# Layer 1's constants and halves prepared inside layer 0, and the last batch's normalisers fetched by two queues

## The chip, the cores and the metric

The kernel runs on one NeuronCore of one Trainium2 chip. The metric is the device time of one execution in microseconds, taken as the median over runs.

## What is computed

Two transformer layers are applied to x of shape (4, 1024, 128), in float32. The reference, cut to what matters:

```python
xn = layernorm(x)
x = x + L0_attn(xn) + L0_ffn(xn)   # 16 heads of 8, one shared key/value; SwitchHead: 8 heads, 8 experts, top 2
xn = layernorm(x)
x = x + L1_attn(xn) + L1_ffn(xn)   # FAVOR+ linear attention; 8 experts, top 2, plus a shared expert
return x
```

In layer 0's attention each head's output is softmax(q k) v, so each head's sum over keys has to be divided by its own denominator before the output projection with Wo. Layer 1's attention needs q, k and v as products of xn with Wq, Wk and Wv, and its experts need to know which tokens chose which expert.

## The kernel before

All 32 tiles of 128 tokens stay in SBUF as `x`, and `xnT` holds the normalised tokens transposed. A product that needs more precision than one float32r pass is made in three (`matmul3`, lines 91 to 98): both operands are split into an upper half (`upper`, a rounded copy) and a lower half (`lower`, what the rounding left, line 86).

**Layer 0** (`layer0`) runs 32 steps, 8 per batch, in one software-pipelined loop whose order is written out by hand for each engine; step i works on one SwitchHead head and two attention heads of batch i // 8. Around that loop each engine has the work of a batch's boundary (`batch_work`). The sums of the attention heads, undivided, go out to DRAM (`store_sums`, on ScalarE's queue), and with them a ninth row, the denominators. When a batch is through:

- `load_dens` (L685, SyncE's queue) fetches the denominators into `dens`, and `invert_dens` (L1369, VectorE) inverts them.
- `load_o` stores the inverses to DRAM (L692), fetches the sums into `o_in` (L699, 16 DMAs) and then the inverses, each repeated over 8 partitions, into `rden_in` (L705, 16 DMAs), all on SyncE's queue. Each of these 32 DMAs brings 32 KB in rows of 256 bytes.
- `divide_o` (L775, GpSimd, two halves) multiplies them into `oT`, `project_out` (L421, TensorE) applies Wo, `add_attn` (L1377, VectorE) adds to `x`, `token_moments` (L1384) takes the statistics, `normalise_out` (L1291), `turn_xo` (L386), `keep_xoT` (L977) and the routing (L431, L1403, `choose_experts`, `mix`) follow.

For batches 0 to 2 this lies beside the steps of the next batch. For batch 3 nothing is left beside it: after the loop every engine has a short tail written out by hand. VectorE's tail is the routing of batch 2 first, and then `invert_dens(B - 1)` and the rest. The halves `xs` of a batch's tokens are made by `upper_x` (ScalarE, L963) and `lower_x` (GpSimd, L86) one batch ahead, for layer 0 only.

**Layer 1** (`main1`) is a second block, entered by all engines together behind a barrier. SyncE issues the loads of 15 constants and weights there (L1717); TensorE, ScalarE and VectorE wait for all 15 (`loaded`). Then VectorE makes the upper halves of the weights (L82, `wh` and `w1`), GpSimd the lower halves (L86), ScalarE and GpSimd the halves `xh` of three batches of tokens (L2303, and L86 with 12 pieces). TensorE's first product is `project_in(0, 0)`, behind `w_split` and `x_split`. In slot 1 of batch 0 it counts the tokens of each expert (`count_places`, L1962 and L1963), and VectorE's `rank_tokens` (L2086 to L2111) gives each token its place; TensorE's next ring buffer waits for that (`ranked`), and so does GpSimd, which sends the rows out (`send_rows`, L2459).

## Time and profile before

| what | us |
|---|---|
| median of 3 runs | 3246.56 |
| lowest and highest of them | 3239.7, 3247.78 |
| the profiled execution's own time | 3217.92 |
| its span | 3216.1 |
| layer 0 ends, layer 1 starts (first DMA of layer 1) | 2643.34 |

The span is the time from the first to the last instruction of the profiled execution; 1.82 us of its own time lie around it. That execution was 28.6 us faster than the median of the runs shown, so differences are worked out within it. The profile's page gives the busy time of each engine over the whole span; the stretch around 2600 to 2680 us is read from the timeline, in order of time, and from windows, which give the same sums for a stretch.

### The profile page before, as it was taken

How to read it: one execution, taken by the hardware profiler on the slowest of the kernel's cores; microseconds unless marked ns; L12 is line 12 of the kernel's file. 1: busy time of each engine (PE TensorE's matmuls, PEld its weight loads, DVE VectorE, ACT ScalarE, POOL GpSimd, SP SyncE). 2: the span in 40 equal slices, each digit the busy share in tenths (PEclk: the TensorE clock that was granted, in tenths of full speed). 3: DMA queues.
4: the chain of work that ended last, by engine and by line, in shares of the span. 5: the costliest groups of instructions: out<-in, count | busy, mean ns of one | idle time of the engine just before them, and what ended most of it. 6: DMA issues, size and time to landing. Idle time of an engine off the chain costs nothing. (4 is left out here: it accounts for less than half of the span.)

```text
span 3216.1 us, 51790 instructions
## 1 busy us (share of the span) xinstructions
PE 3007.4 (94%) x17486; PEld 2085.3 (65%) x17486; DVE 2392.0 (74%) x4547; ACT 1617.6 (50%) x3269; POOL 1840.3 (57%) x2283
## 2 busy tenths in 40 slices
PE   4999999999999999999999999999999937898997
PEld 2666666666666666666666666666666625566674
DVE  7888888888888888888888888888878534144343
ACT  1555555555555555555555555555555612344534
POOL 2556666666666666666666666666666426334330
PEclk7999999999999999999999999999999968899999
DMA  5000000101100011001000110010000021123222
GB/s 165 20 22 22 21 22 22 39 23 34 37 22 23 22 31 31 22 22 35 28 22 22 31 31 25 20 44 25 22 22 21 2 49 58 59 85 105 86 76 84
DMA packets 139561, 124.62 MB, mean 39 GB/s; under 512 B 28122, under 2 KB 121828, under 8 KB 139204
## 3 DMA queue, kind: packets, MB, share of 16 engines
q1 hardware_dynamic: 126836, 88.78, 10.0%
q0 software_dynamic: 10160, 30.17, 3.0%
q10 hardware_dynamic: 2304, 2.36, 0.4%
q8 instruction: 143, 2.34, 0.3%
q14 instruction: 118, 0.97, 0.1%
HBM read 97.48 MB, written 29.30 MB: 39 GB/s over the span
## 5 line engine op out<-in xcount | busy, mean ns | idle before, releaser
L1172 DVE TENSOR_REDUCE m_peaks<-m_ring 128x1 f32<-128x512 f32 x1024 | 640.9, 680 | 116.2 <-PE m_ring L270 110.0
L926 ACT ACTIVATE m_expA<-m_ring 128x512 f32<-128x512 f32 x1024 | 538.6, 602 | 370.9 <-PE m_sums L358 179.5
L817 POOL TENSOR_TENSOR m_vprod<-m_vprod 128x512 f32<-128x512 f32 x256 | 354.9, 1386 | 510.7 <-DVE m_vprod L1185 509.3
L826 POOL TENSOR_TENSOR m_oprod<-m_oprod 128x512 f32<-128x512 f32 x256 | 328.1, 1282 | 282.3 <-DVE m_oprod L1252 282.2
L897 ACT ACTIVATE m_prob<-m_ring,m_negs 128x512 f32<-128x512 f32 x512 | 347.0, 684 | 241.6 <-DVE m_negs L1219 241.4
L321 PE MATMUL m_ring<-m_probT,m_vs 128*128 128x256 f32 x2048 | 467.4, 381 | 0.0
L321 PEld LDWEIGHTS m_ring<-m_probT,m_vs 128*128 128x128 f32 x2048 | 384.5, 190 | 79.5 <-issue 27.2
L1213 DVE TENSOR_REDUCE m_negs<-m_ring 128x1 f32<-128x512 f32 x512 | 340.3, 685 | 93.6 <-PE m_ring L98 93.1
L1252 DVE TENSOR_TENSOR m_oprod<-m_ring,m_go 128x512 f32<-128x512 f32 x512 | 341.3, 685 | 57.6 <-PE m_ring L98 53.7
L1185 DVE TENSOR_TENSOR m_vprod<-m_ring,m_gate 128x512 f32<-128x512 f32 x512 | 336.5, 683 | 46.0 <-POOL m_vs L819 23.9
L907 ACT ACTIVATE m_probT<-m_ring 128x512 f32<-128x512 f32 x512 | 285.0, 598 | 58.0 <-PE m_ring L309 54.3
L309 PEld LDWEIGHTS m_ring<-k_ident,m_prob 128*128 128x128 f32 x2048 | 235.3, 141 | 82.8 <-ACT m_prob L897 31.4
L309 PE MATMUL m_ring<-k_ident,m_prob 128*128 128x128 f32 x2048 | 283.8, 276 | 4.7 <-ACT m_prob L897 3.8
L358 PE MATMUL m_sums<-m_expA,m_v 128*32 128x512 f32 x2048 | 273.2, 605 | 2.0 <-ACT m_expA L926 2.0
L270 PE MATMUL m_ring<-m_ks,m_qs 32*128 32x512 f32 x1024 | 211.8, 491 | 30.8 <-DVE m_qs L1164 28.2
L96 PE MATMUL m_ring<-m_wvs,m_xs 128*128 128x512 f32 x512 | 230.5, 450 | 4.1 <-POOL m_wvs L86 2.8
L96 PE MATMUL m_ring<-m_xs,m_yT 128*128 128x512 f32 x512 | 227.9, 445 | 3.3 <-ACT m_prob L897 0.9
L96 PE MATMUL m_ring<-m_wos,m_ctxT 128*128 128x512 f32 x512 | 224.8, 439 | 5.6 <-ACT m_expA L926 2.0
L343 PE MATMUL m_ring<-m_qs,m_ks 32*128 32x512 f32 x1024 | 205.2, 483 | 11.7 <-DVE m_vprod L1185 8.0
L917 ACT ACTIVATE m_ctxT<-m_ring 128x256 fp32r<-128x256 f32 x128 | 49.1, 384 | 314.6 <-PE m_ring L321 314.6
L98 PE MATMUL m_ring<-m_wvs,m_xs 128*128 128x512 f32 x512 | 203.9, 398 | 0.0
L97 PE MATMUL m_ring<-m_wvs,m_xs 128*128 128x512 f32 x512 | 203.5, 397 | 0.0
(293 smaller groups left out, 5646.9 us busy)
## 6 DMA issues: line engine op xcount, KB each, us to landing
m_wraw<-in_v_w SPq DMA_DIRECT2D x32, 512.0 KB, 4.1
m_qf<-q_dram SPq DMA_DIRECT2D x128, 128.0 KB, 2.7
m_wraw<-in_o_w SPq DMA_DIRECT2D x32, 512.0 KB, 4.2
q_dram<-m_kf SPq DMA_DIRECT2D x24, 256.0 KB, 3.0
listed<-in_pad SPq DMA_DIRECT2D x6, 897.0 KB, 11.8
m_xg<-listed SPq DMA_DIRECT2D x39, 138.0 KB, 2.2
m_rows<-answers SPq DMA_DIRECT2D x8, 512.0 KB, 4.2
sums_dram<-m_sumsT ACTq DMA_DIRECT2D x128, 18.0 KB
```

The source lines that it names most:

```text
L96: pe.matmul(out, wh, xh, start=True, stop=False)
L309: last = pe.transpose(ps[:, c * P:(c + 1) * P], prob[t % 2][:, (4 * h + c) * P:(4 * h + c + 1) * P], ident[:, :])
L321: last = pe.matmul(ps[:, 0:2 * P], vs[n % 2][:, k, :], probT[g % 2][:, k, :], start=(k == 0), stop=(k == TPB - 1))
L817: vchain(pool.tensor_tensor(vprod[:, 0:512], vprod[:, 0:512], vprod[:, 512:1024], ALU.add))
L826: ochain(pool.tensor_tensor(op[:, 0:512], op[:, 0:512], op[:, 512:1024], ALU.add))
L897: act.activation(prob[t % 2][:, c * 512:(c + 1) * 512], ring.home["scores", n, t, c][:, :], ACT.Exp, bias=neg[t % 2], accum_out=den[n % 2] ...
L907: act.activation(probT[g % 2][:, 4 * h:4 * h + 4, (t % 2) * P:(t % 2 + 1) * P], ring.home["probT", n, t, h][:, :].rearrange("p (c q) -> p ...
L926: act.activation(expA[hh][:, c * 512:(c + 1) * 512], ring.home["scT", n, k, hh, c][:, :], ACT.Exp)\
L1172: v.tensor_reduce(peaks[:, t, hh, c:c + 1], ring.home["peaks", n, t, hh, c][:, :], AX.X, ALU.max)\
L1185: v.tensor_tensor(vprod[:, c * 512:(c + 1) * 512].rearrange("p (e d) -> p e d", e=4), ring.home["values", n, t, c][:, :].rearrange("p (e d ...
L1213: v.tensor_reduce(half_neg[:, t % 2, c:c + 1], ring.home["scores", n, t, c][:, :], AX.X, ALU.max, negate=True)\
L1252: v.tensor_tensor(oprod[t % 2][:, c * 512:(c + 1) * 512].rearrange("p (e d) -> p e d", e=4), ring.home["outputs", n, t, c][:, :].rearrange ...
```

## The change

What is done in layer 1 before its first product moves into layer 0. The 15 constants are loaded by SyncE in step 29 (`load_layer1`), into `spare`, a tile that held the normalised tokens `xn` and the gates' scratch before. Their halves are made by VectorE alone in layer 0's tail (`split_layer1`), into `wvs`, which layer 0 no longer needs then. `upper_x` and `lower_x` run once more in layer 0, for batch 0's tokens of layer 1, in steps 28 and 29; those of batches 1 and 2 are made in layer 1, between ScalarE's `keep_kT` and `keep_qT` and behind GpSimd's `square_k`. TensorE, ScalarE and GpSimd start layer 1 without a wait for loads.

For the last batch the inversion comes first in VectorE's tail, the sums are fetched by SyncE without a wait for it, the store of the inverses and half of their loads go to ScalarE's queue, the division is shared by GpSimd and VectorE, and the statistics of a half are taken as soon as that half is added.

```diff
+def layer1_consts(spare):
+
+    at, out = 0, {}
+    for name, rows, shape in (("wraw", P, (3, D)), ("woT", P, (D,)), ("bqk", P, (2,)), ("bv", P, (D,)), ("proj", P, (256,)),
+                              ("pick", P, (256,)), ("half", P, (P,)), ("vmask", P, (2, 32)), ("w2", P, (HT, D)),
+                              ("b1", P, (HT,)), ("b2", EM + 2, (D,)), ("ws1", P, (HID,)), ("rank", P, (P + 17 + NG + NT,))):
+        n = math.prod(shape)
+        view = spare[0:rows, at:at + n]
+        out[name] = view.rearrange("p (a b) -> p a b", a=shape[0]) if len(shape) == 2 else view
+        at += n
+    return out
...
-        st, xn, kf = norm_memory(m), m.sbuf("xn", [P, TPB, D]), m.sbuf("kf", [P, 512])
+        st, xn, kf = norm_memory(m), spare[:, 0:T].rearrange("p (t d) -> p t d", t=TPB), m.sbuf("kf", [P, 512])
         tiny = m.sbuf("tiny", [P, 1])
-        g_v, g_one, g_c, g_other = (m.sbuf(f"g_{n}", [P, 64, ES]) for n in ("v", "one", "c", "other"))
+        g_v, g_one, g_c, g_other = (spare[:, k * 512:(k + 1) * 512].rearrange("p (g e) -> p g e", e=ES) for k in range(2, 6))
...
+        def load_rden(eng, b, parts):
+
+            eng.wait_ge(rden_stored, 16 * (b + 1))
+            rden_of = rden_dram[b % 2].rearrange("(h c) (g u) -> c g h u", c=2, g=HD)
+            for c in parts:
+                for g in range(HD):
+                    rows = slice(64 * c + HD * g, 64 * c + HD * (g + 1))
+                    eng.dma_start(rden_in[rows, :, :], rden_of[c, g, :, :].partition_broadcast(HD)).then_inc(o_loaded, 16)
...
                 def load_o(b):
                     if b not in batches:
                         return
-                    sp.wait_ge(dens_inverted, b + 1)
-                    sp.dma_start(rden_dram[b % 2].rearrange("g (s r) -> g s r", s=4), dens[:, :]).then_inc(rden_stored, 16)
                     if b:
                         sp.wait_ge(o_divided, 2 * b)
                     sums_of = sums_dram[b % 2].rearrange("h (i c) k (g u) -> c g k (h i) u", i=2, g=HD)
...
                         for g in range(HD):
                             rows = slice(64 * c + HD * g, 64 * c + HD * (g + 1))
                             sp.dma_start(o_in[rows, :, :], sums_of[c, g, 0:HD, :, :]).then_inc(o_loaded, 16)
-                    sp.wait_ge(rden_stored, 16 * (b + 1))
-                    rden_of = rden_dram[b % 2].rearrange("(h c) (g u) -> c g h u", c=2, g=HD)
-                    for c in range(2):
-                        for g in range(HD):
-                            rows = slice(64 * c + HD * g, 64 * c + HD * (g + 1))
-                            sp.dma_start(rden_in[rows, :, :], rden_of[c, g, :, :].partition_broadcast(HD)).then_inc(o_loaded, 16)
+                    if b < B - 1:
+                        sp.wait_ge(dens_inverted, b + 1)
+                        sp.dma_start(rden_dram[b % 2].rearrange("g (s r) -> g s r", s=4), dens[:, :]).then_inc(rden_stored, 16)
+                    load_rden(sp, b, range(2) if b < B - 1 else (0,))
...
+                def load_layer1():
+                    sp.wait_ge(xn_turned, 2 * B)
+                    sp.wait_ge(gates_ready, 2 * B)
+                    for dst, src in (
+                        (w["wraw"][:, 0, :], a["wkT"]), (w["wraw"][:, 1, :], a["wqT"]), (w["wraw"][:, 2, :], a["wvT"]),
+                        (w["woT"], a["woT"]), (w["bqk"], a["bqk"]), (w["bv"], a["bv1"].partition_broadcast(P)),
+                        (w["proj"], a["proj"]), (w["half"], a["half"]), (w["pick"], a["pick"]), (w["vmask"], a["vmask"]),
+                        (w["b2"], a["b2"]), (w["ws1"], a["ws1"]), (w["w2"], a["ws2"]), (w["b1"], a["bs1"]), (w["rank"], a["rank"]),
+                    ):
+                        sp.dma_start(dst, src).then_inc(layer1_loaded, 16)
...
+                    if i == N0 - 3:
+                        load_layer1()
...
                 def lower_x(b):
-                    if b not in batches:
+                    if not 0 <= b <= B:
                         return
                     pool.wait_ge(x_upper, b + 1)
-                    lower(pool, xs[b % 2][:, 1, :], xnT[:, b * T:(b + 1) * T], xs[b % 2][:, 0, :]).then_inc(x_ready, 1)
+                    at = b % B * T
+                    lower(pool, xs[b % 2][:, 1, :], xnT[:, at:at + T], xs[b % 2][:, 0, :]).then_inc(x_ready, 1)
...
                 divide_o(B - 1, 0)
-                divide_o(B - 1, 1)
...
                 def upper_x(b):
-                    if b not in batches:
-                        return
-                    act.wait_ge(xnT_made, 2 * (b + 1))
+
+                    if not 0 <= b <= B:
+                        return
+                    if b < B:
+                        act.wait_ge(xnT_made, 2 * (b + 1))
+                    else:
+                        act.wait_ge(xoT_made, 2)
                     if b >= 2:
                         act.wait_ge(scores_made, 2 * TPB * HS * (b - 1))
-                    act.activation(xs[b % 2][:, 0, :].bitcast(F32R), xnT[:, b * T:(b + 1) * T], ACT.Copy).then_inc(x_upper, 1)
+                    at = b % B * T
+                    act.activation(xs[b % 2][:, 0, :].bitcast(F32R), xnT[:, at:at + T], ACT.Copy).then_inc(x_upper, 1)
...
+                act.wait_ge(dens_inverted, B)
+                act.dma_start(rden_dram[(B - 1) % 2].rearrange("g (s r) -> g s r", s=4), dens[:, :]).then_inc(rden_stored, 16)
+                load_rden(act, B - 1, (1,))
                 routing_exps(B - 2)
                 roots(5 + B - 1, slice(NT - TPB, NT))
...
+                def split_layer1():
+
+                    v.wait_ge(layer1_loaded, 16 * n_layer1)
+                    v.wait_ge(values_made, 16 * N0)
+                    halves = Chain(v, halves_step)
+                    upper(v, w["wh"][:, 0, :, :], w["wraw"])
+                    halves(upper(v, w["w1"][:, 0, :], w["ws1"]))
+                    lower(v, w["wh"][:, 1, :, :], w["wraw"], w["wh"][:, 0, :, :])
+                    lower(v, w["w1"][:, 1, :], w["ws1"], w["w1"][:, 0, :])
+                    v.tensor_scalar(w["bqk"], w["bqk"], DN, None, ALU.mult)
+
+                def divide_last():
+
+                    v.wait_ge(o_loaded, 512 * B)
+                    v.wait_ge(out_made, 2 * (B - 1))
+                    v.wait_ge(xo_turned, 2 * (B - 1))
+                    v.wait_ge(xo_stored, 16 * FILLS + 16 * (B - 1))
+                    heads = slice(8, 16)
+                    v.tensor_tensor(oT[:, :].rearrange("p (u h) -> p h u", h=H0)[:, heads, :], o_in[:, heads, :],
+                                    rden_in[:, heads, :], ALU.mult).then_inc(o_divided, 1)
...
-                    v.wait_ge(attn_added, 2 * (b + 1))
+                    v.wait_ge(attn_added, 2 * b + 1 + pair // 2)
...
+                invert_dens(B - 1)
                 keep_routing(B - 2)
                 choose_experts(B - 2)
                 mix(B - 2)
-                invert_dens(B - 1)
-                add_attn(B - 1, 0)
-                add_attn(B - 1, 1)
-                for pair in range(4):
-                    token_moments(B - 1, pair)
+                split_layer1()
+                divide_last()
+                for q in range(2):
+                    add_attn(B - 1, q)
+                    token_moments(B - 1, 2 * q)
+                    token_moments(B - 1, 2 * q + 1)
...
-        xh = [m.sbuf(f"xh{k}", [D, 2, T]) for k in range(3)]
+        xh = [*xs, m.sbuf("xh2", [D, 2, T])]
...
-                pe.wait_ge(loaded, 16 * n_loads)
-                pe.wait_ge(consts_ready, 2)
...
                 def project_in(b, side, out_sem, kept_sem):
-                    if side == 0:
-                        pe.wait_ge(x_split, b + 1)
-                    if b == 0 and side == 0:
-                        pe.wait_ge(w_split, 1)
+                    if b and side == 0:
+                        pe.wait_ge(x_split, b)
...
-                    v.memset(cum[k][:, 0:4], 0.0)
-                v.wait_ge(loaded, 16 * n_loads)
-                upper(v, wh[:, 0, :, :], wraw[:, :, :]).then_inc(consts_ready, 1)
-                v.tensor_scalar(bqk[:, :], bqk[:, :], DN, None, ALU.mult).then_inc(consts_ready, 1)
-                upper(v, w1[:, 0, :], ws1[:, :]).then_inc(consts_ready, 1)
+                    last = v.memset(cum[k][:, 0:4], 0.0)
+                last.then_inc(consts_ready, 1)
...
-                for b in range(B - 1):
-                    upper_x(b)
                 for b in range(B):
                     for u in range(SLOTS):
                         if u == 0:
                             keep_kT(b)
                         if u == 1:
                             keep_qT(b)
+                        if b == 0 and u < 2:
+                            upper_x(u + 1)
...
-                pool.wait_ge(consts_ready, 1)
-                lower(pool, wh[:, 1, :, :], wraw[:, :, :], wh[:, 0, :, :]).then_inc(w_split, 1)
-                pool.wait_ge(consts_ready, 3)
-                lower(pool, w1[:, 1, :], ws1[:, :], w1[:, 0, :]).then_inc(w_split, 1)
...
+                            if b == 0:
+                                lower_x(1)
+                                lower_x(2)
```

**Where the instructions stand.** Line numbers are those of the kernel they belong to. SyncE's queue at layer 0's end before (m_ names are layer 0's tiles; "waits" are semaphores, m0_ those of layer 0):

```order
L685 DMA m_dens<-sums_dram 128x1x128 [waits m0_rden_stored,m0_sums_stored]
L692 DMA rden_dram<-m_dens 128x128 [waits m0_dens_inverted]
L699 DMA m_o_in<-sums_dram 8x16x64 [waits m0_o_divided]
L699 DMA m_o_in<-sums_dram 8x16x64 x15
L705 DMA m_rden_in<-rden_dram 8x16x64 [waits m0_rden_stored]
L705 DMA m_rden_in<-rden_dram 8x16x64 x15
L711 DMA xn_dram<-m_oT 128x1024 [waits m0_xo_ready]
```

and ScalarE's queue at the same place now:

```order
L976 DMA sums_dram<-m_sumsT 9x512 [waits m0_sums_kept]
L1014 ACTIVATE k_xnT<-m_ring 128x512 [waits m0_x_ready,m0_xo_turned] x2
L1185 DMA rden_dram<-m_dens 128x128 [waits m0_dens_inverted]
L264 DMA m_rden_in<-rden_dram 8x16x64 [waits m0_rden_stored]
L264 DMA m_rden_in<-rden_dram 8x16x64 x7
L1057 ACTIVATE m_lg<-m_lg 128x64 [waits m0_lg_ready]
L981 ACT_TABLE_LOAD
L981 ACTIVATE m_rstd<-m_va 128x8 [waits m0_var_ready]
```

The store of the inverses and 8 of the 16 loads of `m_rden_in` left SyncE's queue for ScalarE's, where they stand ahead of batch 2's routing exponential.

VectorE's tail before:

```order
L1411 TENSOR_TENSOR m_t_sel<-m_t_sel,m_t_q 128x64 [waits m0_mix_step]
L1412 TENSOR_TENSOR m_lg<-m_lg,m_t_first 128x64 [waits m0_mix_step]
L1418 TENSOR_TENSOR m_lg<-m_lg,m_t_sel 128x64 [waits m0_lg_exps]
L1419 TENSOR_REDUCE m_t_m<-m_lg 128x8 [waits m0_mix_step]
L1420 RECIPROCAL m_t_m<-m_t_m 128x8 [waits m0_mix_step]
L1421 TENSOR_TENSOR k_combine<-m_lg,m_t_m 128x8x8 [waits m0_mix_step]
L1369 RECIPROCAL m_dens<-m_dens 128x128 [waits m0_dens_loaded]
L1377 TENSOR_TENSOR k_x<-k_x,m_ring 128x512 [waits m0_x_added,m0_out_made] x2
L1384 BN_STATS m_bn<-k_x 128x6 [waits m0_attn_added]
L1384 BN_STATS m_bn<-k_x 128x6
```

and now (k_spare holds the constants, k_wvs the halves):

```order
L1481 RECIPROCAL m_t_m<-m_t_m 128x8 [waits m0_mix_step]
L1482 TENSOR_TENSOR k_combine<-m_lg,m_t_m 128x8x8 [waits m0_mix_step]
L83 CAST k_wvs<-k_spare 128x384 [waits m0_values_made,m0_layer1_loaded]
L83 CAST k_wvs<-k_spare 128x512
L87 TENSOR_TENSOR k_wvs<-k_spare,k_wvs 128x384 [waits m0_halves_step]
L87 TENSOR_TENSOR k_wvs<-k_spare,k_wvs 128x512
L1420 TENSOR_SCALAR k_spare<-k_spare 128x2
L1429 TENSOR_TENSOR m_oT<-m_o_in,m_rden_in 128x8x64 [waits m0_xo_turned,m0_xo_stored,m0_out_made,m0_o_loaded]
L1438 TENSOR_TENSOR k_x<-k_x,m_ring 128x512 [waits m0_x_added,m0_out_made]
L1445 BN_STATS m_bn<-k_x 128x6 [waits m0_attn_added]
```

The reciprocal has gone from behind the routing to ahead of it (it stands 14 instructions before the first row shown), five instructions on the weights and one half of the division came in, and the statistics follow each addition.

ScalarE at the start of layer 1 before:

```order
L2291 UNCONDITIONAL_BRANCH [waits barrier_Pool_Activation_PE_DVE_SP_release]
L2303 ACTIVATE m_xh<-k_xnT 128x1024 [waits m1_consts_ready,m1_loaded]
L2303 ACTIVATE m_xh<-k_xnT 128x1024 x2
L2311 ACTIVATE m_kT<-m_ring,m_bqk 128x1024 [waits m1_kT_made]
L2319 ACTIVATE m_qT<-m_ring,m_bqk 128x1024 [waits m1_qT_made]
L2362 ACT_TABLE_LOAD
```

and now:

```order
L2332 UNCONDITIONAL_BRANCH [waits barrier_Pool_Activation_PE_DVE_SP_release]
L2347 ACTIVATE m_kT<-m_ring,k_spare 128x1024 [waits m1_kT_made]
L2339 ACTIVATE k_xs<-k_xnT 128x1024
L2355 ACTIVATE m_qT<-m_ring,k_spare 128x1024 [waits m1_qT_made]
L2339 ACTIVATE m_xh<-k_xnT 128x1024
L2400 ACT_TABLE_LOAD
```

The copies of the tokens' halves no longer stand ahead of `m_kT`; two of them stand behind `m_kT` and `m_qT`, and no wait for loads is left.

## Rows read from the trace of the kernel before

**Rows 1.** The page of the profile, part 1: busy us, share of the span, instructions.

```profile
PE 3007.4 (94%) x17486; PEld 2085.3 (65%) x17486; DVE 2392.0 (74%) x4547; ACT 1617.6 (50%) x3269; POOL 1840.3 (57%) x2283
```

**Rows 2.** Timeline, end of layer 0: start us, us, engine line op out<-in xcount [idle before].

```profile
2592.84 0.56 SPq L685 DMA_DIRECT2D m_dens<-sums_dram  x1
...
2596.22 0.23 DVE L1403 TENSOR_TENSOR m_lg<-m_ring,m_gb 128x64 f32<-128x64 f32 x1 [2.02 <-PE m_ring L431]
...
2600.38 0.26 ACT L1020 ACTIVATE m_lg<-m_lg 128x64 f32<-128x64 f32 x1 [6.24 <-DVE m_lg L1412]
...
2601.57 0.94 DVE L1369 RECIPROCAL m_dens<-m_dens 128x128 f32<-128x128 f32 x1
...
2602.93 5.84 SPq L699 DMA_DIRECT2D m_o_in<-sums_dram  x16
...
2608.82 5.93 SPq L705 DMA_DIRECT2D m_rden_in<-rden_dram  x16
...
2619.38 2.52 POOL L775 TENSOR_TENSOR m_oT<-m_o_in,m_rden_in 128x512 f32<-128x512 f32 x2 [21.18 <-DMA m_rden_in<-rden_dram]
...
2621.95 3.78 PE L421 MATMUL m_ring<-m_wo,m_oT 128*128 128x128 f32 x16 [25.77 <-POOL m_oT L775]
```

**Rows 3.** DMA issues of 2585:2660: xcount, KB each, median us to landing.

```profile
m_dens<-sums_dram SPq DMA_DIRECT2D x1, 64.0 KB, 2.3
...
rden_dram<-m_dens SPq DMA_DIRECT2D x1, 64.0 KB, 1.6
```

**Rows 4.** DMA issues of 2089:2106 (same transfer, batch 2).

```profile
rden_dram<-m_dens SPq DMA_DIRECT2D x1, 64.0 KB, 4.3
```

**Rows 5.** Windows: us, busy (x instructions) of each engine, PEclk, DMA share, GB/s.

```profile
2093.00:2095.00 2.00, 2.00 (x14) 0.98 (x14) 2.00 (x4) 0.88 (x2) 0.00 (x0) 1.00 0.67 117
...
2614.00:2616.00 2.00, 0.00 (x0) 0.00 (x0) 0.00 (x0) 0.00 (x0) 0.00 (x0) 0.50 0.72 71
...
2700.00:2750.00 50.00, 44.93 (x447) 32.94 (x448) 12.24 (x18) 23.05 (x27) 34.06 (x35) 1.00 0.19 60
```

**Rows 6.** Timeline, VectorE after the last output projection.

```profile
2625.77 0.69 DVE L1377 TENSOR_TENSOR k_x<-k_x,m_ring 128x512 f32<-128x512 f32 x1 [1.02 <-PE m_ring L421]
...
2626.49 2.05 DVE L1384 BATCH_NORM_STATS2 m_bn<-k_x 128x6 f32<-128x128 f32 x8
```

**Rows 7.** Timeline, the start of layer 1.

```profile
2643.34 0.36 SPq L1717 DMA_DIRECT2D m_wraw<-in_wkT  x1
...
2653.13 0.36 DVE L82 CAST m_wh<-m_wraw 128x384 fp32r<-128x384 f32 x1 [7.92 <-DMA m_rank<-in_rank]
...
2656.12 8.63 POOL L86 TENSOR_TENSOR m_xh<-k_xnT,m_xh 128x256 fp32r<-128x256 f32 x12
...
2659.50 0.77 PE L96 MATMUL m_ring<-m_xh,m_wh 128*128 128x512 f32 x1 [21.35 <-POOL m_xh L86]
```

**Rows 8.** Timeline, layer 1's ranking of tokens and what runs beside it.

```profile
2656.48 0.83 DVE L2078 TENSOR_TENSOR m_qpT<-m_qpT 128x256 f32<-128x256 f32 x1
...
2670.12 1.11 ACT L2319 ACTIVATE m_qT<-m_ring,m_bqk 128x1024 f32<-128x1024 f32 x1 [6.56 <-PE m_ring L98]
...
2671.54 0.42 DVE L2086 COPY m_qpT<-m_ring 128x256 f32<-128x256 f32 x1 [2.11 <-PE m_ring L1963]
...
2671.99 2.26 DVE L2089 TENSOR_TENSOR m_qpT<-m_qpT 128x256 f32<-128x256 f32 x5
...
2680.57 0.24 DVE L2111 TENSOR_SCALAR m_weight_rows<-m_owner,m_rank 128x39 uint32<-128x39 f32 x1
```

**Rows 9.** Timeline, GpSimd and SyncE in layer 0.

```profile
1856.92 2.36 POOL L86 TENSOR_TENSOR m_xs<-k_xnT,m_xs 128x1024 fp32r<-128x1024 f32 x1
...
2398.95 0.39 SPq L667 DMA_DIRECT2D m_wraw<-in_v_w  x1
...
2441.90 1.72 SPq L659 DMA_DIRECT2D m_qf<-q_dram  x4
```

More of the change, by code:

```diff
@@ L163, in top2, with layer0 @@
     return sel, q
-def layer0(nc, whole, a, x, xnT, ident, order, combine, choice, xn_dram, listed):
+def layer1_consts(spare):
[8 more added lines that the diff above has]
+    return out
+def layer0(nc, whole, a, x, xnT, ident, order, combine, choice, xn_dram, listed, xs, spare, wvs, w):
     with ExitStack() as ctx:
@@ L195, in layer0 @@
         wraw = m.sbuf("wraw", [D, ES * PS])
[L196 to L197 removed]
+        wos = m.sbuf("wos", [PS, 2, ES * D])
         qf = m.sbuf("qf", [P, T])
@@ L2480, in scatter_answers @@
                                                 yg[j % 2][:, h, :], None).then_inc(scattered[j % 2], 16)
-                for b in range(B - 1):
-                    lower_x(b)
                 for b in range(B):
```

56 lines of the change are left out of this document (23 added, 33 removed).

## The prediction

> **What bounds the kernel now.** Over the whole span TensorE is busy 94% of the time [rows 1], so layer 0's loop is TensorE's, and an edit there that adds work to other engines should cost little. That share is an average over stages, however. The timeline around the border of the two layers shows another stage: TensorE's output projection of the last batch (L421) starts at 2621.95 after 25.77 us of idling, and its first product of layer 1 at 2659.50 after 21.35 us [rows 2, 7]. I read the rows backwards from these two starts. The first waited for the division (POOL L775, 2619.38), which waited 21.18 us for the inverses' loads; those were issued one behind the other from 2602.93 to 2614.75, 32 DMAs on SyncE's queue, and nothing of it could start before the reciprocal at 2601.57, which stood behind the routing of batch 2 on VectorE [rows 2]. The second waited for the 15 loads of layer 1 (first issued at 2643.34, the last landed at 2653.13, the [<-DMA] of that row) and then for the halves, of which GpSimd's twelve pieces take 8.63 us [rows 7]. Both are chains of single steps with all other engines idle, so what is cut from them is cut from the time, until another chain is as long.
>
> **The change, part by part.**
>
> *The sums and the inverses.* The denominators are requested at 2592.84 [rows 2] and land 2.3 us later [rows 3], at 2595.1. The reciprocal, now first on VectorE, takes 0.94 and ends at 2596.1; VectorE waits for TensorE until 2596.22 anyway [rows 2], so nobody behind it is late. ScalarE's queue is free until its exponential of 2600.38 [rows 2]; it stores the inverses at 2596.2. The store lands after 1.6 us alone [rows 3], after 4.3 where other transfers run beside it [rows 4]; here SyncE's loads run beside it but are small, and I take 2.3, so 2598.5. SyncE issues the 16 loads of the sums from 2593.4 at 0.365 us each (5.84 / 16, rows 2), until 2599.2, and its 8 loads of inverses until 2602.2; ScalarE's 8 end at 2601.5.
>
> When the data are there is the disputed term. The same 1 MB took 16.45 us before from the first issue to the division's start (2602.93 to 2619.38), and 4.6 us from the end of the last issue at 2614.75 [rows 2]. If the engines that move the data set the pace, the division starts 16.45 after 2593.4, at 2609.85; if the issues do, 4.6 after 2602.2, at 2606.8. The rows speak for some of each: in the last batch the transfers ran at a busy share of 0.72 and 71 GB/s, less than the 90 GB/s at which 32 KB per 0.365 us are issued, but with room left, and the same transfers of batch 2 ran at 117 GB/s [rows 5]. I take the middle, 2608.3.
>
> VectorE must be ready by then for its half of the division. ScalarE's exponential now stands behind its DMAs, at 2601.5 instead of 2600.38 [rows 2]. Behind it come four small operations (the reciprocal ended 1.9 us after 2600.67 with its own 0.94 in it, so 1.0), then the halves of the weights: two casts (0.36 for the 384 columns of the first, rows 7), two subtractions of 384 and 512 columns at 0.45 per 256 [rows 8], and a small scaling, together estimated at 2.4 us. That ends at 2605.2, hidden behind the loads, by 1.6 us even if the issues set the pace.
>
> The division was two GpSimd pieces in 2.52 us [rows 2], now one piece on each engine. VectorE slows beside GpSimd: the same 256 columns took 0.83 while GpSimd subtracted and 0.45 (2.26 / 5) when it was idle [rows 8]. So 512 columns take it 1.4 to 1.9, and I take 1.5. The projection starts at 2609.8 instead of 2621.95: **-12.1 us**. Bounds: -16.8, if the data come 1.6 after the last issue and the division takes 1.3; -8, if the store takes 4.3, the pace stays 71 GB/s or falls with a second queue, and the division takes 2.
>
> The Trainium skill has a rule against the two queues (page "DMA: Bandwidth & Descriptors", section "Issuing engines are not separate DMA queues"): all of them end in the same 16 DMA engines, and a second issuer saves only the time of issuing. By it the first of the two paces above holds; no row here shows two queues on this transfer.
>
> *The statistics.* Of the 8 pieces that took 2.05 us behind the second addition [rows 6], four now run while TensorE still makes the second half (VectorE idled 1.02 there, rows 6): **-0.9 us**.
>
> *The start of layer 1.* No load, split or wait is left ahead of TensorE's first product, so it starts some 0.1 to 0.2 after the barrier, at 2643.5 instead of 2659.50: **-16.0 us** (bounds -16.1, and -14.5 if the instructions have first to be fetched). What hid behind those waits must be looked at: VectorE's memory sets and marks are wanted only when the first products are through, 10.6 us after the start (2659.50 to 2670.12, rows 7, 8); ScalarE's two copies stand behind `m_kT` and `m_qT` and make the first GELU a little late, while TensorE waits for the ranking anyway.
>
> *The ranking.* It runs on VectorE, 2671.54 to 2680.81, while GpSimd was idle [rows 8]. GpSimd's halves of batch 2 now start when ScalarE has made `m_qT` (ended 2671.23, rows 8) and the upper half, 12.8 us after layer 1's start, and last 2.9; the ranking runs from 12.0 to 21.3 after it. In these 2.9 us VectorE does about half of its work, by the pair 0.83 and 0.45 above: **+1.4 us** (bounds 0 and +2.8).
>
> *In layer 0's loop.* One more ScalarE copy, one more GpSimd subtraction of 2.36 us, and 15 issues on SyncE (at 0.37 us each, as above, some 6 us), put between SyncE's load at 2398.95 and the next one at 2441.90, which waits for TensorE, not for SyncE [rows 9]. Cover: TensorE's 94%. I take 0 (bounds 0 and +3.4: the 2.36 and a copy of about 1 laid bare). The new order of `load_o` for batches 0 to 2 costs nothing: a step of 78 us lies behind each.
>
> Sum: -12.1 - 0.9 - 16.0 + 1.4 = **-27.6 us**. Against the profiled execution that gives 3217.92 - 27.6 = 3190.3. The median of the runs shown is 28.6 higher, and I know no reason why the difference should depend on it: 3246.56 - 27.6 = **3219.0**.
>
> **The rivals.**
>
> *A, the pace of the DMA engines.* The second queue drains nothing faster; the division starts at 2609.85. For: 71 GB/s below the pace of issuing. Against: 117 GB/s in batch 2 [rows 5]. Time: 1.6 more, 3220.6.
>
> *B, the clock comes back sooner.* TensorE's granted clock was 0.50 (1.2 GHz) around 2614 after it had idled [rows 5], and the first products of layer 1 run at it. TensorE's idling ahead of layer 1 shrinks from 21 to 5 us. If the 10.6 us of its first products ran at 2.4 GHz, 5.3 us would go: 3213.7. Against: the small work of layer 0's tail, with similar pauses, never brought the clock up.
>
> *C, a new wait in the tail.* The store of the inverses waits among the loads of the sums for 4.3 us or longer, the two queues disturb each other, and the ranking loses 2.8: all upper bounds together give -8 - 0.9 - 14.5 + 2.8 + 3.4 = -17.2, so 3229.4.
>
> *D, slower than before.* Layer 1's first batch has TensorE busy 44.93 of 50 us at the full clock between 2700 and 2750 [rows 5]. If the earlier start set its pauses so that the granted clock stays at 1.2 GHz there, that work takes up to 44.9 us more: -27.6 + 44.9, 3263.9. It decides from about 28 us of work that lose the full clock. Against: the order of the work and its pauses there stay as they were, and the stall ahead of it changes by 1.4 us.
>
> *E, the change moves the waits instead.* TensorE starts layer 1 early, but the ranking waits for something else that comes as late as before, so the 16.0 are lost, and the tail's term is at its bound of -8: 3246.56 - 8 - 0.9 = 3237.7, within 0.3% of before. Against: each input of the ranking (the combine weights, the marks, the two products) follows the start by the same distance.
>
> **How the numbers follow.** Forecast 0.60, A 0.22, B 0.08, C 0.05, D 0.02, E 0.03. The time is the forecast's, 3219.0. The range 3207 to 3231 goes from all lower bounds (-16.8 - 0.9 - 16.1 - 5.3 = -39.1, so 3207.5) to C's with the scatter of the median; the runs shown lie within 8 us. 0.3% is 9.7 us, about what a measurement of this kernel can tell from no change; forecast, A, B and C are faster than that, E is within it, D beyond it: 0.95, 0.03, 0.02.
>
> **What would show it.** In the changed profile: the reciprocal of the denominators ahead of 2597; the division at 2606.5 to 2610 with a piece on each engine; the projection's start (L421 before) some 12 us earlier; from the barrier to TensorE's first product under 1 us instead of 16; the ranking 10 to 12 us long instead of 9.3; steps 28 to 31 as long as before. The forecast is wrong if the distance between the loop's end and layer 1's ranking shrinks by less than 17 or more than 39 us, or if the later part of layer 1 takes back what it gained.

## The result, and the profile after

The changed kernel takes **3215.22 us** (median of 4 runs, 3213.97 to 3219.4) where the kernel before took 3247.17 beside it (4 runs): ratio 0.9907, 95% interval 0.9893 to 0.9922, so some 30 us faster (25 to 35 by the interval). The forecast was 3219.0, the range 3207 to 3231. The profiled execution took 3213.97, its span 3212.2.

The timeline of the tail of layer 0 (start, length, engine, line; the bracket is the idle time ahead and what ended it), of SyncE's and ScalarE's queues and the engines behind them, against [rows 2]:

```profile
2591.37 0.56 SPq L708 DMA_DIRECT2D m_dens<-sums_dram  x1
...
2591.98 6.80 SPq L720 DMA_DIRECT2D m_o_in<-sums_dram  x16
...
2593.83 0.95 DVE L1409 RECIPROCAL m_dens<-m_dens 128x128 f32<-128x128 f32 x1 [1.12 <-DMA m_dens<-sums_dram]
...
2594.82 0.36 ACTq L1185 DMA_DIRECT2D rden_dram<-m_dens  x1
...
2598.62 2.91 ACTq L264 DMA_DIRECT2D m_rden_in<-rden_dram  x8
...
2598.83 2.88 SPq L264 DMA_DIRECT2D m_rden_in<-rden_dram  x8
...
2603.48 1.16 DVE L87 TENSOR_TENSOR k_wvs<-k_spare,k_wvs 128x384 fp32r<-128x384 f32 x2
...
2606.54 1.02 DVE L1429 TENSOR_TENSOR m_oT<-m_o_in,m_rden_in 128x512 f32<-128x512 f32 x1 [1.82 <-DMA m_rden_in<-rden_dram]
2606.58 2.00 POOL L807 TENSOR_TENSOR m_oT<-m_o_in,m_rden_in 128x512 f32<-128x512 f32 x1 [9.85 <-DMA m_rden_in<-rden_dram]
...
2608.64 3.78 PE L444 MATMUL m_ring<-m_wo,m_oT 128*128 128x128 f32 x16 [13.98 <-POOL m_oT L807]
```

The reciprocal follows its load at once, both queues issue side by side, the halves of the weights fit ahead of the division, and the division starts at 2606.54 on both engines. GpSimd's half takes 2.00 and VectorE's 1.02, so GpSimd's sets the projection's start: 2608.64, 13.3 us earlier than before. 1.5 us of that the loop of this execution gave, whose end (the load of `dens`) came at 2591.37 instead of 2592.84.

The start of layer 1 in the same view, against [rows 7, 8]:

```profile
2629.05 2.26 SPq L1773 DMA_DIRECT2D m_rows<-xn_dram  x3
...
2629.09 0.76 PE L97 MATMUL m_ring<-k_xs,k_wvs 128*128 128x512 f32 x1 [5.24 <-PEq L266]
...
2636.68 1.12 ACT L2355 ACTIVATE m_qT<-m_ring,k_spare 128x1024 f32<-128x1024 f32 x1 [2.58 <-PE m_ring L99]
...
2638.34 0.41 DVE L2127 COPY m_qpT<-m_ring 128x256 f32<-128x256 f32 x1
...
2638.78 3.88 DVE L2130 TENSOR_TENSOR m_qpT<-m_qpT 128x256 f32<-128x256 f32 x5
...
2638.82 3.57 POOL L87 TENSOR_TENSOR m_xh<-k_xnT,m_xh 128x256 fp32r<-128x256 f32 x4 [0.92 <-ACT m_xh L2339]
...
2648.99 0.24 DVE L2152 TENSOR_SCALAR m_weight_rows<-m_owner,k_spare 128x39 uint32<-128x39 f32 x1
...
2649.34 2.09 PE L1844 MATMUL m_ring<-k_spare,m_kT 32*128 32x256 f32 x16 [10.01 <-DVE m_weight_rows L2152]
```

TensorE's first product starts 0.04 us after SyncE's first instruction; before, it came 16.16 later [rows 7]. `m_qT` is made 7.6 us after the start, not 10.6 as I had carried over. The ranking's five additions take 3.88 us beside GpSimd instead of 2.26 alone [rows 8]. It ends at 2649.23, 31.6 us earlier than before's 2680.81.

**But** in this pair of profiles the whole gain is 4 us (3217.92 to 3213.97). Behind the ranking the two traces part. The waits of ScalarE in the changed kernel, window 2650 to 2800 (us in total, times, longest), and the line that sums up by line the chain of work of the same kernel from 2640 to 2800:

```profile
ACT m_hT L2400 <- remote: 9.1, 1, 9.1
ACT m_kshT L2361 <- remote: 4.5, 1, 4.5
```

```profile
by line: another core or an unknown queue 14.5%; PE m_ring L1997 13.5%; issue 12.0%; PE m_ring L1966 5.3%; PE m_ring L1999 4.8%; PE m_ring L1844 4.2%; PE m_kv_sums L1899 4.0%; PE m_ring L1881 3.6%; PE m_ring L1949 3.6%; PE m_ring L1884 3.2%
```

These are waits in which the profile sees nobody who is late; before's profile has none there. I call these waits stalls. Read as a pair, the two profiles say that the change makes stalls that eat the gain. The runs say 30 us. One of the two is misread, so the first question of the experiments is whose the stalls are.

For all kernels below I take the same five distances from the profile, one execution of each kernel: from the load of `dens` to the projection; from there to layer 1's first DMA; to the ranking's end; to VectorE's first `m_oT` in layer 1 (the end of its first batch); and to the end of the span. All are in us, worked out from the starts in the timeline.

| kernel | profiled run | 1: to projection | 2: to layer 1 | 3: to ranking's end | 4: to first m_oT | 5: to the end |
|---|---|---|---|---|---|---|
| before (shown above) | 3217.92 | 29.11 | 21.39 | 37.47 | 99.28 | 436.0 |
| changed | 3213.97 | 17.27 | 20.41 | 20.18 | 128.49 | 434.5 |
| before_again | 3245.72 | 32.51 | 21.40 | 37.97 | 125.92 | 433.7 |
| after_again | 3212.97 | 15.79 | 20.40 | 23.43 | 126.71 | 434.5 |
| tail_only | 3227.51 | 16.91 | 20.41 | 37.95 | 124.99 | 434.7 |
| prep_only | 3229.13 | 30.19 | 21.40 | 20.19 | 124.77 | 435.1 |
| after_third | 3192.58 | 16.85 | 20.41 | 20.25 | 99.30 | 436.1 |
| one_queue | 3189.27 | 20.33 | 20.40 | 23.01 | 99.30 | 434.1 |
| late_halves | 3181.36 | 17.08 | 20.41 | 17.83 | 97.01 | 434.0 |
| sync_sends | 3187.46 | 16.63 | 20.42 | 20.25 | 99.91 | 436.5 |
| sync_sends_2 | 3190.82 | 17.83 | 20.41 | 20.23 | 99.28 | 436.2 |
| sync_sends_3 | 3191.03 | 18.56 | 20.41 | 23.44 | 99.34 | 435.1 |
| warm | 3191.49 | 23.85 | 17.89 | 18.52 | 102.36 | 434.1 |
| best | 3174.60 | 16.07 | 21.34 | 15.89 | 98.17 | 428.6 |

### The profile page after: what moved, and what is told of

It reads as the page before. It is cut to its first block and busy times, and to the rows that moved or that the text cites. A ratio compares the mean times of both kernels' runs of the same rounds, so it can differ in the third digit from the quotient of the medians.

```text
span 3212.2 us, 51788 instructions
## 1 busy us (share of the span) xinstructions
PE 3015.0 (94%) x17486; PEld 2087.3 (65%) x17486; DVE 2399.2 (75%) x4550; ACT 1616.1 (50%) x3269; POOL 1836.4 (57%) x2277
## 5 line engine op out<-in xcount | busy, mean ns | idle before, releaser
L332 PEld LDWEIGHTS m_ring<-k_ident,m_prob 128*128 128x128 f32 x2048 | 235.6, 141 | 83.3 <-ACT m_prob L929 31.6
L293 PE MATMUL m_ring<-m_ks,m_qs 32*128 32x512 f32 x1024 | 213.5, 493 | 31.6 <-DVE m_qs L1204 29.0
L97 PE MATMUL m_ring<-k_wvs,k_xs 128*128 128x512 f32 (+1 forms) x536 | 236.3, 441 | 2.8 <-POOL k_wvs L87 1.6
L97 PE MATMUL m_ring<-k_xs,m_yT 128*128 128x512 f32 x512 | 226.8, 443 | 3.4 <-ACT m_prob L929 0.9
L366 PE MATMUL m_ring<-m_qs,m_ks 32*128 32x512 f32 x1024 | 205.1, 482 | 10.9 <-DVE m_vprod L1225 6.9
L99 PE MATMUL m_ring<-k_wvs,k_xs 128*128 128x512 f32 (+1 forms) x536 | 210.6, 393 | 0.0
L98 PE MATMUL m_ring<-k_wvs,k_xs 128*128 128x512 f32 (+1 forms) x536 | 209.3, 390 | 0.0
```

The costliest lines, as they stand in the source:

```text
L97: pe.matmul(out, wh, xh, start=True, stop=False)
L332: last = pe.transpose(ps[:, c * P:(c + 1) * P], prob[t % 2][:, (4 * h + c) * P:(4 * h + c + 1) * P], ident[:, :])
```

## The experiments

The kernels were timed in four sets, each on one chip, with the kernel before timed on the same chip. It took 3244.04 (23 runs), 3215.11 (11), 3220.04 (9) and 3243.82 (7). Its runs lie from 3238.9 to 3250.9 on the first and the fourth chip and from 3210.3 to 3225.6 on the other two, so these are chips of two kinds.

### The first set: whose stalls, and the two parts alone (before at 3244.04)

`before_again` and `after_again` are the two kernels, unedited.

> The kernel before, unchanged, so the time is 3240 to 3250. The question is its trace. The changed kernel's trace has four stretches in layer 1's first batch in which the engines wait for something the profile doesn't name (9.7 us at 2657, 6.1 at 2688, 4.5 at 2696, 9.1 at 2723); the one profile of before, 3217.92, has none and spends 27 us less there. Theory 1 (they belong to both kernels, and the profiled execution of before was a rare one without them): this profile is at 3240 to 3250 and has 20 to 30 us of such waits between the ranking and the first load of listed rows. Theory 2 (the change makes them): this profile has none in layer 1's first batch, which is then as short as in the first profile, and the 28 us between profile and runs lie elsewhere, in layer 0 or around the span.

> The changed kernel, unchanged: 3214 to 3219. Both theories expect the stalls in its layer 1 again. If this profile has none, and is at 3187 to 3192, the stalls come and go in both kernels, whatever the change does.

Measured: before_again 3242.21 (ratio 0.9995, 0.9986 to 1.0004), after_again 3216.07 (**0.9915**, 0.9898 to 0.9933). The longest waits in the chain of before_again, window 2680 to 2800 (start, length, what):

```profile
2692.67 9.63 another core or an unknown queue
...
2707.75 3.94 another core or an unknown queue
...
2723.07 6.08 issue
...
2730.87 4.46 another core or an unknown queue
...
2755.05 10.20 another core or an unknown queue
```

The kernel before has the same stalls on this chip, 34.3 us in these five (some of it beside work that would have run anyway), and distance 4 is 125.92 instead of 99.28. Theory 1 of the expectation holds so far as the stalls are not the change's. Its second half, that before's first profile was a rare execution, is not what the later sets suggest: at 3217.92 it lies among the runs of the chips without stalls and outside all 23 of this chip, so it most likely came from a chip of the other kind. Of the 28.6 us between that profile and the median of the runs, these stalls make 26.6 by distance 4.

`tail_only` is the kernel before with the change's tail and without its preparation of layer 1: the new `load_o`, `load_rden`, `divide_last` and the new order of the tail; `prep_only` is the changed kernel with these undone (both cut to the order of the calls):

```
 # tail_only (from before)              # prep_only (from the changed kernel)
+invert_dens(B - 1)                     -invert_dens(B - 1)
 keep_routing(B - 2)                     keep_routing(B - 2)
 choose_experts(B - 2)                   choose_experts(B - 2)
 mix(B - 2)                              mix(B - 2)
-invert_dens(B - 1)                     +invert_dens(B - 1)
+divide_last()                           split_layer1()
...                                     -divide_last()
+load_rden(act, B - 1, (1,))            -load_rden(act, B - 1, (1,))
```

> Only the part on the last batch's sums (inversion first, two queues, shared division, statistics between); layer 1 starts as before. By the prediction's terms -13.0 us against before: 3234. By the trace of the changed kernel -11.8 - 0.9: 3234 to 3235. If the parts depend on each other (the shorter pause ahead of layer 1 is what brings TensorE's clock back sooner), this part alone also takes the 21 us pause of before into layer 1 and gives no more than that.

> Only layer 1's constants and halves prepared in layer 0; the last batch's sums as before. By the prediction's terms -16.0 + 1.4 = -14.6: 3232.5. If the clock comes back sooner ahead of the ranking here too (rival B): 3 to 5 less, 3228 to 3230. Theory 2 above (the change makes the stalls, through TensorE's earlier start in layer 1): the stalls are here, and not in the kernel with the tail alone.

Measured: tail_only 3228.73 (0.9952, 0.9939 to 0.9964: -15.6 by the ratio), prep_only 3235.44 (0.9967, 0.9957 to 0.9977: -10.7). The stalls are in both (distance 4 is 124.99 and 124.77), as they are in before_again, so theory 2 falls. The distances split cleanly: the tail's edit moves 1 and 2 alone, the preparation 3 alone, each by as much as both do together. The two ratios add up to -26.3 and both parts gave -27.6 on this chip. Each part missed its expected time: tail_only was some 5 us faster than the 3234 and prep_only 3 us slower than the 3232.5 (5 to 7 slower than the 3228 to 3230 expected if rival B happens, which it did in its profile). In microseconds prep_only gained less than its distance 3 (-17.8). Its eleven runs lie from 3227 to 3241, and in the profiled one a step of layer 0 took 85.8 us (2050.32 to 2136.12, from one load of `qf` to the next) where before_again's took 83.0 (granted clock 0.83 against 0.91 from 2070 to 2090). What remains of the difference I can't name.

### The second set: one queue, the ranking, the stalls, the clock (before at 3215.11)

`one_queue` gives ScalarE's 8 loads back to SyncE:

```
-load_rden(sp, b, range(2) if b < B - 1 else (0,))
+load_rden(sp, b, range(2))
-load_rden(act, B - 1, (1,))
```

> The changed kernel, but SyncE issues all 16 loads of the inverses and ScalarE only the store (against 3214 to 3219). If the issues set the pace of this transfer (the division 4.6 to 5 us after the last issue), 8 more issues of 0.36 us make the division 2.9 us later, and the time 2.9 more. If the 16 DMA engines do (rival A), the division comes at the same time as with two queues, and the time is the same within 0.5 us.

Measured: 3190.78, ratio 0.992 (0.9904 to 0.9936). The rows in the timeline:

```profile
2598.37 6.16 SPq L264 DMA_DIRECT2D m_rden_in<-rden_dram  x16
...
2608.55 1.02 DVE L1428 TENSOR_TENSOR m_oT<-m_o_in,m_rden_in 128x512 f32<-128x512 f32 x1 [7.52 <-DMA m_rden_in<-rden_dram]
```

The division comes 4.0 us after the last issue (2604.53), as with two queues (4.8 in the changed kernel's profile: 2601.71 to 2606.54). Distance 1 is 20.33, against 17.1 as the mean of the eight profiles with two queues and no idle products, which lie from 15.79 to 18.56. From the first issue of the sums to the division, those eight take 13.1 to 15.8 us, mean 14.4, and this one 17.6; the three with the old tail took 16.45, 17.51 and 19.84. If the DMA engines set the pace, one queue or two would make no difference. **The issues set the pace, in the main**, and the second queue is worth about 3 us, by one profile without it. Not all of the pace is theirs: the time from the last issue to the division lies between 3.4 and 6.1 us over all profiles but this one, and one issue took from 0.36 to 0.52 us (8.25 for 16 in before_again), which nothing here explains. The times of different chips are too coarse to show it.

`late_halves` moves GpSimd's halves:

```
 if u == 0:
     square_k(b)
-    if b == 0:
-        lower_x(1)
-        lower_x(2)
...
     send_rows(2 * u - 1)
+if b == 0 and u in (3, 6):
+    lower_x(u // 3)
```

> The changed kernel, but GpSimd subtracts the halves of batches 1 and 2 behind its third and sixth pair of row sends, not ahead of the ranking. If VectorE's ranking is 1.6 us longer because GpSimd works beside it, the stretch from the second copy of the projections to the ranking's end falls from 12.5 back to 10.7 to 11.0, and the time by 1.6 at most. If the subtractions then run beside VectorE's maxima, they take that back: no change.

Measured: 3183.04, ratio 0.9905 (0.9888 to 0.9921). VectorE's rows:

```profile
2639.31 0.42 DVE L2127 COPY m_qpT<-m_ring 128x256 f32<-128x256 f32 x1 [0.31 <-PE m_ring L2007]
2639.77 2.26 DVE L2130 TENSOR_TENSOR m_qpT<-m_qpT 128x256 f32<-128x256 f32 x5
```

The five additions are back at 2.26, the ranking takes 9.3 us instead of 10.9, distance 3 falls from 20.2 to 17.8. So the cost that I set at 1.4 us is real, and is 1.6 in the ranking and 2.4 with what lies ahead of it. Distance 4 is 2.3 us shorter too (97.01), which I did not expect and did not follow up. The ratio cannot show either.

`sync_sends` takes the row sends away from GpSimd, whose `send_rows` issues them as indirect DMAs. It also puts rows and answers down in their own order, one behind the other, so both reach other places than the reference's:

```
+sp.dma_start(listed[at:at + P, :], rows[...])
...
-pool.indirect_dma_start(answers[:, :], bass.IndirectOffsetOnAxis(target[...], 0), yg[...], None)
+pool.dma_start(answers[(2 * j + h) * P:(2 * j + h + 1) * P, :], yg[...])
...
-send_rows(2 * u - 2)
-send_rows(2 * u - 1)
```

> The changed kernel, but the 64 tables of rows are sent in their own order by SyncE as plain DMAs, instead of to their places by GpSimd's indirect DMAs, and the answers too are put down in order (so rows reach other places than they should). It asks what the stalls of layer 1's first batch hang on. Theory 1, GpSimd's own work of sending holds up signals between the other engines: no stall beside the sends, from the ranking's end to the first load of listed rows 115 to 122 us as in the first profile of before instead of 143 to 147, so some 24 us faster, 3190 to 3195. Theory 2, the traffic or TensorE's clock does it: 143 to 147 as before.

Measured: 3188.55 (0.9917, 0.99 to 0.9934), distance 4 99.91. It told nothing: on this chip one_queue and late_halves, which send by GpSimd, have no stall either (99.30, 97.01).

`warm` adds products that nobody reads:

```
+def keep_busy(n):
+    for _ in range(n):
+        pe.matmul(sums[:, :], ident[:, :], xnT[:, 0:512], start=True, stop=True)
+pe.wait_ge(sums_kept, N0)
 routing(B - 2)
+keep_busy(22)
 project_out(B - 1, 0)
 ...
```

> The changed kernel with products that nobody reads, on TensorE while it waits: 22 ahead of the last projection, 8 behind it, 6 at layer 0's end, 18 beside the ranking. Rival B says that layer 1's start is paced by TensorE's clock. If the clock stays up, the projection takes 1.9 instead of 3.78, the turns 1.05 instead of 2.14, the last routing 1.9 instead of 3.58, the first products of layer 1 2 to 4 us less: 7 to 9 us less together, 3206 to 3210. If these products come in the way of the real ones instead (they are too many, or their waits are late), each place costs up to its own length, 1 to 3 us.

Measured: 3193.34, ratio 0.9937 (0.9921 to 0.9952). The change alone was not timed on this chip; on two others it had 0.9915 and 0.9903, so the idle products gave nothing and probably cost some. TensorE's rows:

```profile
2596.21 20.83 PE L642 MATMUL m_sums<-k_xnT,k_ident 128*128 128x512 f32 x44
...
2616.87 1.95 PE L444 MATMUL m_ring<-m_wo,m_oT 128*128 128x128 f32 x16
...
2618.66 7.03 PE L642 MATMUL m_sums<-k_xnT,k_ident 128*128 128x512 f32 x16
...
2625.52 1.04 PE L409 MATMUL m_ring<-k_ident,m_oT 128*128 128x128 f32 x8
...
2627.30 1.95 PE L454 MATMUL m_ring<-m_gw,k_xnT 128*128 128x8 f32 x16 [0.74 <-ACT k_xnT L1022]
```

Both halves of the expectation came true. The projection takes 1.95 instead of 3.78, the turns 1.04 instead of 2.14, the routing 1.95 instead of 3.58 (the longer times are those of before's and of the changed kernel's profile). But one idle product takes 0.95 us (20.83 / 22, a part of it at half clock) and 0.88 where the granted clock is 1.00 throughout (7.03 / 8), about twice what I had counted. So the 22 end 6.5 us after the division and the real work waits: distance 1 is 23.85. The 18 beside the ranking end 3.5 us after it (2656.79 and 2653.28), and distance 4 is 102.36, 3 us longer.

### The third set: the change where there are no stalls, and the best version (before at 3220.04)

> The changed kernel, unchanged, once more, because the second set of runs met before at 3215 where the first had it at 3244. Either before is at 3244 here, then this is at 3214 to 3217 and its profile takes 143 to 147 us from the ranking's end to the first load of listed rows. Or before is at 3215, then this is at 3186 to 3188 and that stretch 116 to 118 us. In both the ratio stays at 0.991 to 0.992: what the change gives does not depend on the stalls.

Measured: **3187.02, ratio 0.9903** (0.9889 to 0.9917), distance 4 99.30. The change gives as much where there are no stalls: 30.5 us come from the distances 1 to 3 against the first profile of before, and 31.2 by the ratio.

`best` is late_halves with 12, 4, 5 and 7 idle products.

> The changed kernel with the halves of batches 1 and 2 behind the row sends, and with fewer of the idle products than before (12, 4, 5 and 7; one takes 0.95 us and not the 0.47 that the first count supposed). Against late_halves, which gave 3183 where before had 3215: 4.5 us less from the projection to layer 1's start, 1.7 or more less until the ranking, 1 less behind it. 3175 to 3178 where before has 3215 (ratio 0.988), 3205 where before has 3244. If the idle products bring nothing, it is at late_halves' ratio, 0.9905.

Measured: 3185.18 (3174.6 to 3190.89, 5 runs), ratio 0.9896 (0.988 to 0.9913). It beats the kernel before, but is not shown to beat the changed one (0.9903 beside it). Both ratios of its expectation, 0.988 with a gain from the idle products and 0.9905 without, lie in the interval. Its profiled run was its fastest, 3174.6, with distance 3 at 15.89; distance 2 is 21.34, because the last routing ran at half clock again (3.58) and the five products behind it came in the way. The clock was not held with this few. Distance 5 is 428.58, some 5 us under late_halves' 434.0; in its first 20 us the granted clock is 0.92 instead of 0.74. Whether the idle products brought that is not shown: `warm`, with more of them, has 434.1.

> The kernel with plain row sends by SyncE once more. Where before is at 3244 (stalls): theory 1, GpSimd's indirect sends hold up the other engines, says 115 to 122 us from the ranking to the third batch's start and 3186 to 3190, ratio 0.983; theory 2 (traffic, clock) says 143 to 147 and a ratio of 0.991. Where before is at 3215 both say 3188, and the question stays open.

Measured: 3190.27 (0.9908, 0.9891 to 0.9924), again on a chip without stalls, so the question stayed open.

### The fourth set: the stalls (before at 3243.82)

> The plain row sends by SyncE a third time, for the question on the stalls alone; the last two chips had none in any kernel. Where before is at 3244: theory 1 (GpSimd's indirect sends hold up the other engines) says no stall in layer 1's first batch, 3186 to 3191, ratio 0.983; theory 2 (traffic or clock) says stalls of 25 us and 3213 to 3217, ratio 0.991. Where before is at 3215 to 3220, both say 3187 to 3191, and the question stays open.

Measured: **3191.3, ratio 0.9836** (0.9815 to 0.9857). Before is at 3244, as in the first set, and this kernel has no stall: distance 4 is 99.34, where with GpSimd's sends it was 124.8 to 126.7 on the other chip on which before takes 3244. No kernel with GpSimd's sends was profiled on this chip, so that it has stalls there is read from its time. Its waits of ScalarE, window 2655 to 2800:

```profile
ACT m_hT L2412 <- PE m_ring L99: 38.3, 7, 12.8
ACT m_qpT L2403 <- PE m_ring L1965: 25.3, 4, 13.8
...
ACT m_kshT L2373 <- PE m_ring L1880: 2.8, 1, 2.8
```

No wait of the kind "remote" is left. Theory 1 holds: the stalls go when the rows are no longer sent by GpSimd's indirect DMAs, on chips of one kind. Theory 2 is left with little: the same amount of rows goes out here, in less time (64 sends in 39 us), and TensorE's clock came back as late in this profile as in after_again's, which has the stalls. How the sends hold up the others is not settled. Of the four waits for "another core or an unknown queue" in before_again, the three that begin at 2692.67, 2730.87 and 2755.05 end 1.5 to 2.2 us after the last send of a group; the fourth, 3.94 us from 2707.75, ends inside a group. The last of them, in ScalarE's and GpSimd's rows:

```profile
2753.76 1.28 ACT L2362 ACT_TABLE_LOAD   x1
2765.27 1.26 ACT L2362 ACTIVATE m_hT<-m_ring,m_b 128x512 f32<-128x512 f32 x2 [10.22 <-remote]
```

```profile
2760.80 0.96 POOL L2459 DMA_INDIRECT listed<-m_rows,m_place  x1 [0.31 <-issue]
2762.07 0.96 POOL L2459 DMA_INDIRECT listed<-m_rows,m_place  x1 [0.30 <-issue]
```

The last send of the group ends at 2763.03, ScalarE goes on at 2765.27. The sends themselves are not slower on such a chip: 0.96 us with 0.30 between them, as in before's first profile. Whether it is the offsets of the indirect form, any DMA that GpSimd issues, or the scattered places that the rows go to was not tried on such a chip, and the edit changes all three.

## Why the prediction was right

Measured by the means over the profiles in the table (old tail: three; new tail: eight, without one_queue, warm and best; for distance 3 three without the preparation and eight with it, without late_halves, warm and best):

| term | predicted | measured |
|---|---|---|
| sums, inverses, division (distance 1) | -12.1 (-16.8 to -8) | 30.6 to 17.1: -13.5 |
| statistics (distance 2) | -0.9 | 21.39 to 20.41: -1.0 |
| layer 1's start and ranking (distance 3) | -16.0 + 1.4 = -14.6 | 37.8 to 20.2, in three of eight profiles to 23.0 to 23.4: -17.6 or -14.5, mean -16.4 |
| layer 0's loop | 0 (0 to +3.4) | 0 to +0.2: see below |

The mechanism was the forecast one, two chains of single steps. By the distances the terms add up to -30.9, by the ratios the change gave 30.2 beside the first result, 27.6 and 31.2 in the sets, against the forecast's 27.6. The parts of the forecast that missed are these.

**Sums and inverses.** I took the middle between two paces, 2608.3. one_queue showed that in the main the issues set the pace; in the changed kernel's profile the division came 4.8 us after the last of them, against 4.6 in the row of before that I used. Rival A, the pace of the DMA engines, falls: it wanted 16.45 us from the first issue to the division, and the profiles with two queues have 13.1 to 15.8. The rule that I cited for it (the Trainium skill, page "DMA: Bandwidth & Descriptors", section "Issuing engines are not separate DMA queues") is not contradicted: it grants a second issuer the time of issuing, and here that time was most of the bound, 2.9 us of issues for 3.2 us measured in one profile. My step from the rule to rival A's price was wrong, because I let it decide between the paces, which it doesn't. Two sizes were off too, and took up what the middle had too much: SyncE's loads were issued at 0.425 us each and not at 0.365 (6.80 / 16), and the division took 2.1 us and not 1.5. There I had the wrong engine slowed: VectorE's half took 1.02, little more than twice the 0.45 of 256 columns, and GpSimd's took 2.00 where before one of its two took 1.26 (2.52 / 2). So the projection came 17.1 us after the load, as good as the 17.0 of the forecast, and that is in part luck. That the gain was 1.4 us more than forecast lies in the kernel before: its row that I used has 29.11, the mean of the three profiles with the old tail is 30.6 (29.11 to 32.51). The store took 3.8 us and not 2.3 (2594.82 to 2598.62), which cost nothing, since SyncE was issuing the sums until 2598.78.

**Layer 1's start.** The 16 us are there to 0.1 us: the first product starts 0.04 us after layer 1's first DMA. No row stood behind the bound of -14.5, for instructions that have first to be fetched, and no profile shows such a time. Behind that start rival B, to which I gave 0.08, happened in five of eight profiles. The windows of the changed kernel, and of after_again below it (busy time of PE, PEld, DVE, ACT, POOL; granted clock; DMA share; GB/s):

```profile
2630.00:2634.00 4.00, 4.00 (x20) 3.53 (x19) 2.02 (x9) 1.97 (x2) 0.78 (x1) 0.61 0.95 251
2634.00:2638.00 4.00, 4.00 (x24) 3.56 (x24) 2.75 (x6) 1.42 (x3) 3.90 (x5) 1.00 0.59 144
```

```profile
2630.00:2634.00 4.00, 4.00 (x21) 4.00 (x21) 0.00 (x0) 1.57 (x2) 3.29 (x4) 0.50 1.03 261
2634.00:2638.00 4.00, 4.00 (x12) 3.24 (x12) 1.98 (x10) 0.81 (x1) 1.35 (x2) 0.50 0.00 1
```

In the first the granted clock is back at 2.4 GHz some four us after the start at 2629.05, in the second it is at 1.2 GHz for over eleven from 2626.53; distance 3 is 20.18 and 23.43. The granted clock of all eight profiles shows the same two cases, and nothing between them. In the three profiles without the preparation it came back over 11 us after the first product. The step that failed is the one that set B against the forecast as one case in twelve: I argued that the work of layer 0's tail never brought the clock up. In the changed kernel's profile it did, behind the projection (granted clock 1.00 from 2613 to 2615, 0.50 again by 2617), and so in three of the other profiles. B is a second outcome of many executions, worth 3.2 us and not the 5.3 that I gave it; what decides between the two is not shown. The measured 3215.22 lies nearer to B's 3213.7 than to the forecast's 3219.0.

**The ranking.** +1.4 was +1.6 in the ranking itself.

**Layer 0's loop.** The end of the loop moves between executions of the same code: the load of `dens` comes at 2590.33 to 2597.85 in the eleven profiles with the preparation and at 2590.79 to 2592.84 in the three without it. The stretch that the preparation touches is steadier. From the fifth-last load of `qf` to the load of `dens` the three without it take 459.4, 459.6 and 460.7 us, nine of the eleven with it 459.4 to 459.6, the other two 460.9 and 463.2. So the loop hides the added work, as forecast, in all but perhaps these two.

**Rivals C, D and E** did not happen: no term reached its upper bound, the full clock was not lost behind the ranking where there were no stalls (distance 4 is 99.3 in both kernels), and the ranking's inputs followed the start.

**The open sentence** is one that the prediction had only in passing: that I knew no reason why the 28.6 us between the profiled execution and the runs should depend on the change. They did not, but I did not know their source either. It was 25 to 29 us of stalls on the chips of the timed runs, in one stretch that the change moves but does not touch. That they are the same for both kernels was luck, not knowledge. The forecast's own test ("if the later part of layer 1 takes back what it gained") would have called the change worthless from the pair of profiles alone.

## What to carry to other kernels

A profile and the timed runs may come from chips of different kinds. When they disagree by more than the runs scatter, find the stretch that holds the difference (here by profiling the kernel before a second time) ahead of any comparison with a changed kernel, or a stall of the chip is booked to the change. In a chain of many small DMAs count the issues: at 0.36 to 0.52 us each they were most of the bound here, and a second queue gave back about its share. And before filling pauses with idle products to hold the clock, measure one of them: at twice the guessed length they cost here as much as the clock gave, or more.

## What was not expected of the hardware

- On chips of one kind other engines waited for 4 to 10 us at a time while GpSimd issued groups of indirect sends (25 to 29 us in all, in five profiles), with nobody late in the profile; on two other chips the same sends had none. With the rows sent by SyncE, on a second chip on which the kernel before takes 3244, it was gone (3191.3 beside 3243.82).
- The same start of layer 1 gets TensorE's full clock back some 4 us or over 11 us after it, in six and three of the nine profiles with the preparation and no idle products, and its ranking ends 3.2 us earlier or later with it. The changed kernel itself, profiled three times, shows both.
- An unread fp32 product of 128x512 takes 0.88 us at the full granted clock (eight in 7.03 us).
